# Fifth layer of a six-layer network: first mixing term on another engine, and the order of VectorE's steps in a round

## The reference, cut to what matters

```python
x = x + _L1_attn_ref(_layernorm(x), ...)          # fifth layer
# inside, with the axes (length, batch, width) read as the unit reads them:
xn = (q - mu) / jnp.sqrt(var + EPS) * ln_g + ln_b
u = silu(xn @ Wu.T + bu); v = silu(xn @ Wv.T + bv); base = silu(xn @ Wb.T + bb)
quad_q, quad_k = mk(qqw, qqb), mk(qkw, qkb)       # base * weight + bias, rotated
quad_qk = einsum('bgne,bgme->bgnm', quad_q, quad_k)
kernel = square(relu(quad_qk / CHUNK + bias))     # kept where m <= n
quadratic = einsum('bgnm,bgme->bgne', kernel, vch)
out = (u * (linear + quadratic)) @ Wo.T + bo + shortcut
```

## Time and profile before

| | us |
|---|---|
| median of 3 runs | 1437.73 |
| lowest, highest | 1432.18, 1439.77 |
| the profiled execution | 1445.08 |
| its span | 1441.4 |

### The profile page before, as it was taken

The page is one execution under the profiler, slowest core; times in us unless marked ns, Lnnn a source line. Parts: engine busy times, 40 slices in busy tenths (PEclk is TensorE's granted clock), DMA queues, the critical chain, the costliest instruction groups (busy, mean ns, idle before and its releaser), DMA issues.

```text
span 1441.4 us, 21161 instructions
## 1 busy us (share of the span) xinstructions
PE 739.2 (51%) x6133; PEld 591.6 (41%) x6141; DVE 811.5 (56%) x2467; ACT 494.0 (34%) x1097; POOL 607.5 (42%) x581
## 2 busy tenths in 40 slices
PE   4212572147745223631454999327677453999400
PEld 3211362026645112531422888314445322888400
DVE  7786245367775771454571556438878571556422
ACT  4000132144424001331302778325454301778300
POOL 3741645314443006546406664360441106664376
PEclk9999786567975555875555999758777755999755
DMA  8210252000002002521101334110110001235222
GB/s 234 71 46 8 57 82 64 25 0 1 0 3 59 1 0 50 80 71 49 44 0 45 79 79 66 50 43 8 35 32 15 23 1 42 74 78 70 56 74 75
DMA packets 85443, 68.06 MB, mean 47 GB/s; under 512 B 11146, under 2 KB 76682, under 8 KB 85378
## 3 DMA queue, kind: packets, MB, share of 16 engines
q0 software_dynamic: 14432, 29.46, 11.1%
q1 hardware_dynamic: 70946, 37.81, 9.1%
HBM read 39.96 MB, written 27.26 MB: 47 GB/s over the span
## 4 chain that ended last, share of the span: by engine, by line
PE 37%; DVE 28%; issue 14%; POOL 10%; another core or an unknown queue 5%; ACT 4%; DMA 3%; DVEq 0%; POOLq 0%; ACTq 0%
POOL rt L937 8%; PE bank L546 4%; PE bank L548 4%; PE bank L507 3%; PE bank L568 3%; PE bank L565 3%; PE bank L547 3%; PE bank L566 3%; DVE rt L714 3%; PE bank L533 2%; DVE stats L321 1%; PE bank L360 1%; DVE nwt L269 1%; DVE srch L710 1%
## 5 line engine op out<-in xcount | busy, mean ns | idle before, releaser
L919 POOL DMA_INDIRECT turned<-xrows_moe,token x256 | 263.7, 1030 | 336.3 <-DVE token L805 200.3
L937 POOL DMA_INDIRECT rt<-y_moe,slot_i x192 | 183.1, 954 | 152.0 <-DMA y_moe<-arena 87.4
L621 ACT ACTIVATE turned<-bank,b1T 128x256 f32<-128x256 f32 x320 | 125.4, 475 | 180.0 <-PE bank L548 129.4
L821 DVE TENSOR_TENSOR turned<-turned 128x1024 bf16<-128x1024 f32 (+1 forms) x128 | 130.5, 1020 | 52.2 <-ACT turned L625 39.1
L565 PE MATMUL bank<-w2h,turned 128*128 x832 | 145.5, 227 | 12.2 <-issue 11.0
L566 PE MATMUL bank<-w2h,turned 128*128 x832 | 145.2, 227 | 7.0 <-issue 6.8
L546 PE MATMUL bank<-rt,w1h 128*128 128x256 bf16 x416 | 122.2, 294 | 41.3 <-issue 31.2
L828 DVE COPY arena<-bank 128x256 f32<-128x256 f32 x128 | 54.1, 423 | 138.3 <-remote 82.1
L568 PE MATMUL bank<-w2l,turned 128*128 x832 | 120.8, 226 | 14.7 <-issue 14.4
L862 DVE SCALAR_TENSOR_TENSOR x<-rt,small,x 128x128 f32<-128x128 f32 x192 | 61.9, 349 | 114.2 <-DMA rt<-y_moe,slot_i 106.4
L613 ACT ACTIVATE turned<-bank 128x512 f32<-128x512 f32 x48 | 28.7, 598 | 281.0 <-PE bank L548 219.2
(11 more groups left out here) (278 smaller groups left out, 1860.8 us busy)
## 6 DMA issues: line engine op xcount, KB each, us to landing
y_moe<-arena SPq DMA_DIRECT2D x128, 128.0 KB
xrows_moe<-arena SPq DMA_DIRECT2D x12, 512.0 KB, 3.2
turned<-xrows_moe,token POOLq DMA_INDIRECT x256
rt<-y_moe,slot_i POOLq DMA_INDIRECT x192
x<-in_x SPq DMA_DIRECT2D x4, 512.0 KB, 6.0
arena<-in_w SPq DMA_DIRECT2D x1, 2048.0 KB, 9.4
arena<-in_w SPq DMA_DIRECT2D x8, 256.0 KB, 4.5
xrows_moe<-w2h SPq DMA_DIRECT2D x8, 256.0 KB
```

The lines of the kernel that those rows point to most:

```text
L621: last = nc.scalar.activation(s["h32"][:, k % 2, o], bank[1 + 2 * (k % 2) + u // 2][:, W * (u % 2):W * (u % 2) + W], ACT.Gelu, bias=b1T[:, ...
L821: nc.vector.tensor_tensor(s["hl16"][:, k % 4], s["h32"][:, r], s["hh"][:, k % 4], ALU.subtract)\
L919: nc.gpsimd.indirect_dma_start(out=s["xs"][:, 2 * (t % BODY) + j], out_offset=None, in_=s["xdram"], in_offset=bass.IndirectOffsetOnAxis(ap ...
L937: nc.gpsimd.indirect_dma_start(out=ytok[:, at % TOK], out_offset=None, in_=s["ydram"], in_offset=bass.IndirectOffsetOnAxis(ap=slot_i[:, k, ...
```

## The change

Two things change in the fifth layer. First, the four scalings for m = 0 leave VectorE; ScalarE makes them in a new step `first_terms`, which stands behind `heads` on ScalarE and waits for the kernel (`kern`), the values (`uv`) and the buffer of z (`zt`). VectorE's mixing, now a function `mix` of its own, waits for them (`z0`). Second, VectorE's iteration is written in another order: combine, add, low, kernel, moments, mixing, where it was combine, add, moments, low, kernel, mixing.

```diff
+            def first_terms(j):
+                act.wait_ge(au["uv"], B * (j + 1))
+                act.wait_ge(au["kern"], j + 1)
+                if j >= 2:
+                    act.wait_ge(au["zt"], j - 1)
+                for n in range(B):
+                    nc.scalar.activation(z[:, j % 2, n], uv[:, j % 2, 0, 0:EH], ACT.Identity,
+                                         scale=kern[:, 3, OFF[n]:OFF[n] + 1]).then_inc(au["z0"], 1)
...
                 if 0 <= j + 1 < NJ:
                     heads(j + 1)
+                    first_terms(j + 1)
                 if 0 <= j - 1 < NJ:
                     norms6(j - 1)
...
-                done(nc.vector.tensor_tensor(kk, r, r, ALU.mult))
+                nc.vector.tensor_tensor(kk, r, r, ALU.mult).then_inc(au["kern"], 1)
+                dve.wait_ge(au["kern"], j + 1)
+
+            def mix(j):
+                par = j % 2
                 dve.wait_ge(au["uv"], B * (j + 1))
-                if j >= 2:
-                    dve.wait_ge(au["zt"], j - 1)
-                for m in range(B):
+                dve.wait_ge(au["z0"], B * (j + 1))
+                for m in range(1, B):
                     for n in range(m, B):
                         i = OFF[n] + m
-                        v, w, zn = uv[:, par, m, 0:EH], kk[:, i:i + 1], z[:, par, n]
-                        if m == 0:
-                            last = nc.vector.tensor_scalar(zn, v, w, None, ALU.mult)
-                        else:
-                            last = nc.vector.scalar_tensor_tensor(zn, v, w, zn, ALU.mult, ALU.add)
+                        zn = z[:, par, n]
+                        last = nc.vector.scalar_tensor_tensor(zn, uv[:, par, m, 0:EH], kk[:, i:i + 1], zn, ALU.mult, ALU.add)
                     done(last)
...
                 if six is not None:
                     add(six)
-                scales(five, six)
                 if 0 <= j + 2 < NJ:
                     low(j + 2)
                 if 0 <= j + 1 < NJ:
                     heads(j + 1)
+                scales(five, six)
+                if 0 <= j + 1 < NJ:
+                    mix(j + 1)
```

More of the change, by code:

```diff
@@ L1222, in program @@
         au = sems("gau", "stat", "chain", "scal", "norm", "moved", "turned", "copied", "high", "low", "b", "bs", "uvp", "uv",
-                  "qkp", "qkc", "dve", "z", "zt", "ztc", "o", "add", "rb", "sel", "rows")
+                  "qkp", "qkc", "dve", "kern", "z0", "z", "zt", "ztc", "o", "add", "rb", "sel", "rows")
         l6 = sems("logits6", "stat", "scal", "norm", "turned", "copied", "lg", "lgc", "hl", "xrow0", "xrow1")
```

## The result

| | before | changed |
|---|---|---|
| median, us | 1438.6 (4 runs, 1432.18 to 1439.77) | 1483.01 (4 runs, 1481.83 to 1487.31) |
| span of the profiled execution | 1441.4 | 1484.2 |
| round 0 to 6, us | 16.5, 18.5, 22.8, 22.8, 22.7, 19.9, 18.0 | 19.4, 21.5, 29.2, 28.6, 27.7, 29.1, 23.4 |
| kernel 0 to kernel 7 | 141.2 | 178.9 |
| kernel 7 to the sixth layer's first reduction (L660) | 31.8 | 37.6 |

The ratio is 1.0305 (95% interval 1.0276 to 1.0335): 44 us slower, 1487 were forecast. Nothing changed outside the layer: the stretch behind it is as long as before, and kernel 0 starts at 979.10 against 978.97. In the whole layer VectorE's busy time stayed nearly the same (141.75 us from 965 to 1200, against 140.85), so the added time is waiting.

A forecast was written before the change was run, and what follows sets the result against it. No single engine bounds the kernel; who waits decides, with VectorE's and ScalarE's lines nearly level. Rounds 43.7 plus tail 5.4 make 49.1 us more, added to the 1437.73 median: 1487, range 1471 to 1499.

The forecast's parts named there:

- the tail: From kernel 7 to ScalarE's norms for group 6: 20.0 us instead of 14.6, so 5.4 us more.
- the heads' slack: Fifth layer, later rounds: ScalarE's heads are ready only 0 to 3 us before VectorE's kernel needs them.
- The ring: Fifth layer: heads, kernel, moments, credit, norms, next heads follow in turn; 184.9 us from kernel 0 to 7, 43.7 more.
- rounds 1 and 6: Fifth layer: 24.4 us for round 1, including 1.7 for outputs at a lower clock, and 26.2 for round 6.
- Rival A: Fifth layer: TensorE stays at the lower clock for whole rounds, about 8 us more, 1495; chance 0.14.
- Rival B: Fifth layer: only the gather's line lengthens, 4.5 us in each of rounds 2 to 6, so 1460; chance 0.07.
- Rival C: Fifth layer: VectorE's own work is the bound, so moving the scalings makes it faster, 1428 to 1433; chance 0.03.
- Kernels right behind the heads: In the changed timeline, each VectorE kernel starts right after ScalarE's heads copy ends, idle before it, in all rounds.
- One sign: In the changed timeline, gathers no longer end last: L862 is done before VectorE waits.
- The wait for the credit: ScalarE's wait grows from 1 to 3 us to some 6 us in rounds 2 to 4, less the activations.
- Part (1): Four scalings move to ScalarE activations: 1.9 us for four (1.6 to 2.4), costing nothing in most rounds.
- Part (4): Earlier low step on VectorE and TensorE's values gain nothing: zero, or 0.6 us a round on the gather's line.

The follow-up runs named there:

- e4: Kernel before, with GpSimd's rows of the sixth layer one group later, so gathers stand behind an earlier group's rows: 1304.09 against 1315.35 us, ratio 0.9914.
- e5: Changed kernel, with GpSimd's rows of the sixth layer one group later: 1475.21 us, 1.3 us less than the changed kernel on that chip.
- e7: Changed kernel, with ScalarE's turned z ahead of the sixth layer's norms and TensorE's outputs ahead of its turned rows: 1464.38 us, 12 us less than the changed kernel.
- e8: Changed kernel, with GpSimd's rows one group later and turned z and outputs ahead of norms and turned rows: 1456.26 us, 20 us less than the changed kernel.
- e2: Changed kernel with VectorE's old order, first terms still on ScalarE right behind the heads: 1350.63 us against 1315.35 for the kernel before, ratio 1.0263.
- e10: Kernel before, with GpSimd's rows later, turned z and outputs earlier, and first terms at the end of ScalarE's iteration: 1299.0 us, ratio 0.9883 to before.
- e1: Changed kernel with VectorE's new order kept, but the first terms back on VectorE: 1354.6 us against 1315.35 for the kernel before, ratio 1.0301.
- e11: Changed kernel, with GpSimd's subtraction (L1297) done for only 1 of 128 columns: 1356.72 us against 1315.26 for the kernel before, ratio 1.0325.
- after_again: The changed kernel unaltered, run again on another chip as a base: 1476.47 us against 1431.42 for the kernel before, ratio 1.0325.

## Why the prediction was right, point by point

**What bounds the kernel.** The reading held: no engine's busy time, but two lines of nearly equal length per round, the gathers' and ScalarE's. In rounds 2 to 4 e4, e5, e7 and e8 each came out as these two lengths say, to within 2.5 us; their totals also hold what the clock (e4) and the tail (e7, e8) gave. One reading was narrow: the heads' slack, given as 0 to 3 us, was 3.8 us before kernel 5 (heads ready at 1078.52, kernel 5 at 1082.28). And the prediction left a mechanism out: it gave the activations no cost of their own ahead of the norms, which holds only because the order closes the ring as well. In the old order the same place costs 35 us (e2).

**The ring, round by round.** Forecast and measured (changed kernel, then its repetition):

| round | 0 | 1 | 2 | 3 | 4 | 5 | 6 | sum | tail to norms 6 |
|---|---|---|---|---|---|---|---|---|---|
| forecast | 20.1 | 24.4 | 28.4 | 29.8 | 27.6 | 28.4 | 26.2 | 184.9 | 20.0 |
| measured | 19.4 | 21.5 | 29.2 | 28.6 | 27.7 | 29.1 | 23.4 | 178.9 | 20.1 |
| again | 18.3 | 22.6 | 28.4 | 27.6 | 29.1 | 28.5 | 22.8 | 177.4 | |

The tail is from kernel 7 (1158.03) to ScalarE's norms for group 6 (1178.10). The four middle rounds sum to 114.2 forecast and 114.6 measured; singly they missed by up to 1.2 us both ways, so that close a sum is partly luck. With the tail the forecast was 49.1 us more; the profiled execution shows 42.8 more of span, the medians 44.4.

**The terms that were too large** are rounds 1 and 6, 2.9 and 2.8 us, nearly the whole miss of 6 us in the sum. For round 1 I had added 1.7 us for outputs at the lower clock. That part came true (L1387 at 1005.57 took 3.62 us). But I had carried the values and heads that follow over at their old duration, and they ran at the full clock this time: from ScalarE's L1420 to the heads' end they took 9.6 us in round 1 (12.6 before) and 6.3 in round 6 (8.3 before). In the kernel before the clock in these values was, in rounds 1 and 6:

```profile
1000.00:1004.30 4.30, 3.91 (x11) 1.79 (x12) 4.16 (x10) 1.69 (x4) 0.00 (x0) 0.50 0.01 2
1112.00:1117.00 5.00, 4.78 (x15) 1.93 (x15) 4.05 (x27) 2.25 (x4) 0.00 (x0) 0.62 0.01 2
```

and in the changed kernel:

```profile
1015.00:1019.00 4.00, 4.00 (x24) 2.66 (x23) 0.18 (x1) 3.08 (x6) 0.00 (x0) 1.00 0.00 0
1152.00:1156.00 4.00, 4.00 (x20) 1.98 (x20) 0.00 (x0) 2.77 (x5) 0.00 (x0) 1.00 0.00 0
```

The third number from the right is the granted clock: 0.50 and 0.62 against 1.00. A stretch taken over from another time of the kernel carries the clock that it had there; the sum of nine such pieces is good to a few us, not better.

**Rival A** (lower clock for whole rounds, 1495) did not come: the mean clock of the layer fell from 0.75 to 0.71, but no round had a mean clock under 0.65, and rounds 1 and 6 had more of the full clock where TensorE worked. **Rival B** fell with e5. **Rival C** (faster) fell with the result, and e10 shows more: even with VectorE as the bound the offload gained nothing. The Trainium skill ("Perfetto Trace Analysis", Optimizing Scalar/DVE Operations) says that it may make sense to offload when VectorE is saturated. At 89% busy that came near, and here it didn't pay: the mixing waited for the activations 2.1 us a group, more than the 1.1 to 1.3 us that were taken off.

**What I said would show it.** Kernels right behind the heads: in all rounds but 3, where kernel 4 (1077.78) stands behind low, with the heads ready at 1077.75. Distances of 28 to 30 in rounds 2 to 5: 27.7 to 29.2. One sign was wrong: L862 was not done before VectorE waits. It waited 24 times for gathers, 27.2 us in all, because they start behind the same late credit; in rounds 2 to 4 VectorE's low step, behind them, ended 0 to 1.5 us before the heads. The wait for the credit came in two pieces: ScalarE waited 3.95 us for the kernel and, behind the activations, 2.38 for the credit, 6.3 in all; some 6, less the activations, were given.

**Part (1)**, the activations: 1.9 us forecast, 1.70 measured, between the bounds of 1.6 and 2.4. The estimate of 1.7 us by the Trainium skill ("ScalarE: Activation LUTs", What ACT_TABLE_LOAD costs) agrees with the row. **Part (4)**, low and the values, gained nothing that shows: kernel 0 starts where it did, and rounds 2 to 5 are as long as forecast without it.

## What to carry to other kernels

Before an instruction is moved behind another one on an in-order engine, ask what each of the two releases on other engines, and walk from the release forward until you come back to the engine you started from: if the walk returns, everything on it adds up in every round. Here the moments released seven steps on two engines that led back to the kernel; behind the kernel they cost 39 us (e1), and an activation that waits for the kernel, put ahead of steps that don't, cost 35 by itself and 7 in a place where it had nothing to wait for. And when two lines are level, a fix of one shows almost nothing (1 us) until the other is shortened too (8 us more).

## What the runs showed of the hardware

VectorE and GpSimd got in each other's way. In the changed kernel the mixing moved beside GpSimd's rows; GpSimd's subtraction (two inputs, 128x512) ran from 1059.91 to 1061.12, and VectorE's product, which starts at 1060.15, took 0.84 us longer, close to the 0.97 us that the subtraction still had to go:

```profile
1058.95 0.89 POOL L1295 CAST w2h<-xn 128x512 bf16<-128x512 f32 x1 [16.34 <-ACT xn L1466]
...
1059.91 1.21 POOL L1297 TENSOR_TENSOR w2h<-xn,w2h 128x512 bf16<-128x512 f32 x1
...
1061.28 1.78 POOL L937 DMA_INDIRECT rt<-y_moe,slot_i  x1 [0.15 <-issue]
```

e11 showed the subtraction to be the cause. The length fits a wait: running at half speed beside the subtraction would have cost the product about 0.5 us, by estimate from the 0.97 us of overlap. The Trainium skill ("SBUF — State Buffer", SBUF: two separate sides) says that a VectorE operation with two inputs in SBUF and a GpSimd operation that reads SBUF exclude each other on a shared pair of ports for the whole instruction. The rows of this product agree. It cost nothing here (the rounds of e11), since the mixing stood behind the credit; in a round that VectorE ends it could cost 0.84 us each time, which no run shows. The first gather behind it took 1.78 us where others of its kind took 0.94 to 1.2; it lay beside the product's last 0.93 us. In e11 it lay beside the product for 1.04 us and took 1.91. That fits a wait of GpSimd for VectorE, the other way round, but no run took the product away from it, so it is argued and not shown.

The chips differ more than the edit: before took 1315 us on two of them and 1431 to 1439 on the other two, while the changed kernel's rounds agreed within 1.5 us. The 120 us lie outside the layer. The changed kernel took 214.7 us from kernel 0 to the sixth layer's first reduction on the chip of after_again and 214.8 on that of e11, but kernel 0 started at 970.74 and 873.55, and the end came 286.7 and 265.8 us behind that reduction. What makes the other stretches longer is open.
